# Attention with routed experts on one core: a reciprocal split by a product with ones, epsilon on POOL, loads in pieces, and value products in two groups

## What is computed

```python
x = x + xattn(layernorm(x), ctx, pos, pos, Wq, Wkv, Wout, bout)
x = x + ffn(layernorm(x), gate_w, bias, shared_w1, shared_w3, shared_w2, w1, w3, w2)
# xattn: q = rope(x @ Wq), k = rope(ctx @ Wk), v = ctx @ Wv
#        softmax(q k^T / 4) v @ Wout + bout       per batch and head
# layernorm: (x - mean) / sqrt(var + 1e-5)
```

## Time and profile before

| | us |
|---|---|
| median of 3 runs | 675.25 |
| lowest and highest | 674.48, 675.48 |
| the profiled execution | 673.13 |
| its span, first to last instruction | 671.4 |
| busy: PE, DVE, POOL, ACT | 613.1 (91%), 491.8 (73%), 378.6 (56%), 371.0 (55%) |

### The profile page before, as it was taken

How to read it: one execution, slowest core, us unless ns; L and a number is a source line. 1 busy time by engine, 2 the same in 40 slices (tenths; PEclk the granted TensorE clock), 3 DMA queues, 4 the chain that set the end, 5 groups by cost and what they waited for, 6 DMA issues and landing times.

```text
span 671.4 us, 17296 instructions
## 1 busy us (share of the span) xinstructions
PE 613.1 (91%) x6016; PEld 366.1 (55%) x6016; DVE 491.8 (73%) x944; ACT 371.0 (55%) x620; POOL 378.6 (56%) x423
## 2 busy tenths in 40 slices
PE   2587889999999999779999999999989999999991
PEld 0244445555555555455656566666656666666660
DVE  7478879999999998766476937667655776776771
ACT  4265636666666666764411126666655765765760
POOL 4856657777777776522000013567557477777662
PEclk9879989999999999989999999999999999999996
DMA  8735745555655446513332822765887955446842
GB/s 300 226 68 98 207 91 131 128 124 129 124 126 128 120 111 159 114 50 120 133 95 93 310 96 76 210 192 95 235 258 201 257 93 88 79 90 164 247 83 34
DMA packets 108882, 95.37 MB, mean 142 GB/s; under 512 B 72544, under 2 KB 77152, under 8 KB 108832
## 3 DMA queue, kind: packets, MB, share of 16 engines
q1 hardware_dynamic: 97184, 68.15, 36.8%
q0 software_dynamic: 8752, 20.71, 15.7%
q10 hardware_dynamic: 2896, 5.85, 2.5%
HBM read 70.12 MB, written 23.07 MB: 139 GB/s over the span
## 4 chain that ended last, share of the span: by engine, by line
PE 78%; DVE 6%; DMA 5%; issue 4%; POOL 3%; ACT 1%; SPq 1%; POOLq 0%; DVEq 0%; ACTq 0%
PE p_sc L754 14%; PE p_sc L723 13%; PE p_qk L723 12%; PE p_qk L538 9%; PE p_v L538 9%; PE p_pv L625 5%; PE p_sc L586 3%; PE p_sc L607 3%; PE p_tr L717 2%; PE p_pv L741 2%; DMA used_twice_too<-used_twice 2%; PE p_sc L610 2%; DMA xeT<-xn2T_dram 1%; DMA xe<-xn_dram,from_at 1%; DVE negmax L1128 1%
## 5 line engine op out<-in xcount | busy, mean ns | idle before, releaser
L1128 DVE TENSOR_REDUCE negmax<-p_sc 128x4 f16<-128x512 f32 x128 | 81.0, 683 | 19.0 <-PE p_sc L586 18.3
L849 ACT ACTIVATE prob<-p_sc 128x512 f32<-128x512 f32 x128 | 69.5, 600 | 24.7 <-PE p_sc L610 20.6
L980 ACT CAST hiddenT<-p_pv 128x384 f16<-128x384 f32 x54 | 25.8, 478 | 99.5 <-PE p_pv L741 99.5
L1530 POOL COPY from_at<-from_rows 128x1 uint32 (+1 forms) x40 | 31.7, 791 | 80.2 <-DVE from_rows L1375 76.9
L1550 POOL DMA_INDIRECT out<-prob,to_at x38 | 68.2, 1796 | 10.8 <-issue 10.4
L754 PE MATMUL p_sc<-used_twice,hiddenT 128*128 128x512 f16 (+1 forms) x306 | 71.7, 379 | 0.0
L723 PE MATMUL p_qk<-used_twice,xeT 128*128 128x352 f16 x420 | 68.4, 313 | 0.2 <-DMA xeT<-xn2T_dram 0.2
L723 PE MATMUL p_sc<-used_twice,xeT 128*128 128x352 f16 x420 | 68.4, 312 | 0.0
L1255 DVE TENSOR_TENSOR hidden<-p_sc,act_g 128x352 f32<-128x352 f32 x55 | 28.8, 524 | 51.2 <-PE p_sc L723 29.1
L959 ACT COPY xeT<-p_tr 128x1024 f16<-128x1024 f16 x40 | 40.5, 1012 | 37.0 <-PE p_tr L717 37.0
L538 PE MATMUL p_qk<-used_twice,xnT 128*128 128x512 f16 x192 | 53.7, 407 | 5.5 <-DVE used_twice L1097 3.8
(11 more groups left out here) (178 smaller groups left out, 1417.9 us busy)
## 6 DMA issues: line engine op xcount, KB each, us to landing
w<-e SPq DMA_DIRECT2D x20, 1408.0 KB
w<-e SPq DMA_DIRECT2D x20, 512.0 KB
out<-stream SPq DMA_DIRECT2D x17, 256.0 KB, 2.5
values<-weighed SPq DMA_DIRECT2D x32, 128.0 KB, 2.0
xn_dram<-xn_parts SPq DMA_DIRECT2D x16, 256.0 KB, 2.0
xn2T_dram<-xn2T SPq DMA_DIRECT2D x16, 256.0 KB, 2.2
w<-e SPq DMA_DIRECT2D x20, 192.0 KB
xeT<-xn2T_dram SPq DMA_DIRECT2D x14, 256.0 KB, 2.7
```

The costliest lines, as they stand in the source:

```text
L849: act.activation(prob[:, c % RING, :], p_scored(c)[:], ACT.Exp, scale=SCALE).then_inc(exp_ready, 1)
L1128: dve.tensor_reduce(negmax[:, c % 2, at:at + CH], p_scored(c)[:].rearrange("p (h t) -> p h t", t=P), AX_X, ALU.max, negate=True).then_inc( ...
L1530: pool.tensor_copy(from_at[:, par, u:u + 1], from_rows[:, bass.ds(q, 1)]).then_inc(from_copied, 1)
```

## The change

- `sums_invert`: the high part is the product of the reciprocal with a tile of fp16 ones instead of a maximum with itself.
- `ln`: DVE no longer adds epsilon. POOL adds it from a constant tile and then takes the power, with a wait between the two. The DVE memsets in `ln` go to columns of their own.
- x is loaded in three pieces: batches 4 and 5 (512 KB) where the one DMA was, 6 to 10 (1280 KB) at the end of ACT's pass 2, and 11 to 15 (1280 KB) at the end of its pass 3.
- The shared expert's weights come in seven pieces over passes 4 to 7: 352 KB of w13 in each and 256, 256 and 192 KB of w2 in the first three.
- For batch 0 only, `q_sum` and `q_low` run on DVE in pass 1, right behind `q_turn`, and no longer on POOL in pass 2.
- Before the first pass DVE makes all four low chunks of wq and turns the first k after them.
- On PE, `shifted_scores` 2 stands ahead of the second half of the value projection, `shifted_scores` 3 behind it, then `weigh_values` 0 and 1 back to back; `weigh_values` 2 and 3 are back to back behind chunk 1 of the query projection.

```diff
-                pe.wait_ge(ln1_step, b * 4 + 4)
+                pe.wait_ge(ln1_step, b * 3 + 3)
...
                 on(-3, spread_recip)
+                on(-2, shifted_scores, 2)
                 on(-1, project_v, 1)
-                on(-2, shifted_scores, 2)
+                on(-2, shifted_scores, 3)
                 on(-2, weigh_values, 0)
-                on(-2, shifted_scores, 3)
                 on(-2, weigh_values, 1)
                 on(0, project_q, 0)
                 on(-5, xn2_transpose)
                 on(-1, scores, 0)
+                on(0, project_q, 1)
                 on(-2, weigh_values, 2)
-                on(0, project_q, 1)
                 on(-2, weigh_values, 3)
...
-            act.dma_start(stream[:, 4:B, :], x_t[:, 4:B, :]).then_inc(x_late, 16)
+            act.dma_start(stream[:, 4:6, :], x_t[:, 4:6, :]).then_inc(x_late, 16)
...
-                if isinstance(b, int) and b == 4:
+                if isinstance(b, int) and 4 <= b < 4 + KC:
                     act.wait_ge(w_lo, KCC + 2 * KC)
-                    act.dma_start(w13[:, 0], s13.rearrange("(c p) n -> p c n", p=P)).then_inc(w_shared, 16)
-                    act.dma_start(w2[:, 0, 0:2, :], s2[0:2 * P].rearrange("(c p) n -> p c n", p=P)).then_inc(w_shared, 16)
-                    act.dma_start(w2[0:ICH[2][1], 0, 2, :], s2[2 * P:INNER]).then_inc(w_shared, 16)
+                    act.dma_start(w13[:, 0, b - 4], s13[(b - 4) * P:(b - 3) * P]).then_inc(w_shared, 16)
+                if isinstance(b, int) and 4 <= b < 4 + len(ICH):
+                    i, k = ICH[b - 4]
+                    act.dma_start(w2[0:k, 0, b - 4], s2[i:i + k]).then_inc(w_shared, 16)
+                if isinstance(b, int) and b in (2, 3):
+                    rows = slice(6, 11) if b == 2 else slice(11, B)
+                    act.dma_start(stream[:, rows, :], x_t[:, rows, :]).then_inc(x_later[b - 2], 16)
...
-                    dve.wait_ge(step, base + 2)
-                    dve.tensor_scalar(mv[:, 1:2], mv[:, 1:2], EPS, None, ALU.add).then_inc(step, 1)
...
+            def q_sum(b, par):
+                dve.wait_ge(turned_q, b * 3 + 3)
+                dve.tensor_tensor(rot[:, 0:DIM], rot[:, 0:DIM], swp[:, 0:DIM], ALU.add).then_inc(q_rot, 1)
+
+            def q_low(b, par):
+                dve.wait_ge(q_hi, b + 1)
+                dve.tensor_tensor(q_part[:, :, :, 1, :], twice_each(rot[:, 0:DIM]), q_part[:, :, :, 0, :], ALU.subtract).then_inc(q_parts, 1)
...
-                dve.tensor_tensor(recip16[0:HEADS], recip[:], recip[:], ALU.max).then_inc(recip_step, 1)
+                if not later(b, 1):
+                    dve.wait_ge(consts, 1)
+                dve.tensor_tensor(recip16[0:HEADS], recip[:], ones16[0:HEADS, :], ALU.mult).then_inc(recip_step, 1)
...
-            weights_low(wq16, wq_in, range(2), KCC)
+            weights_low(wq16, wq_in, range(KC), KCC)
             k_turn(0, 0)
-            weights_low(wq16, wq_in, range(2, KC), KCC)
...
                 on(-1, q_turn)
+                if isinstance(b, int) and b == 1:
+                    q_sum(0, 0)
+                    q_low(0, 0)
...
+                pool.tensor_tensor(to[:], mv[:, 1:2], eps_of[:], ALU.add).then_inc(eps_added, 1)
+                pool.wait_ge(eps_added, b + 1)
+                pool.tensor_tensor(to[:], to[:], minus_half[:], ALU.pow).then_inc(ready, 1)
...
-            pipeline(step, pool, 0, B + 5, 8, (B - 8) // 2, ahead=[rstd1_make, ctx_low])
+            pipeline(step, pool, 0, B + 5, 8, (B - 8) // 2, ahead=[rstd1_make, ctx_low, q_sum, q_low])
```

More of the change, by code:

```diff
@@ L114, in build @@
         ones16 = sb("ones16", [P, P], F16)
-        carrier_dve, carrier_pool = sb("carrier_dve", [P, 1]), sb("carrier_pool", [P, 2 * SUB + 1])
-        minus_half = sb("minus_half", [P, 1])
+        carrier_dve, carrier_pool = sb("carrier_dve", [P, 3]), sb("carrier_pool", [P, 2 * SUB + 1])
+        minus_half = sb("minus_half", [P, 1]); eps_of = sb("eps_of", [P, 1])
         angle = sb("angle", [P, B, ROT])
@@ L871, in xn2_high @@
             def xn2_high(b, par):
-                act.wait_ge(ln2_step, b * 5 + 5)
+                act.wait_ge(ln2_step, b * 4 + 4)
                 if later(b, 1):
@@ L891, in split_shared13 @@
             def split_shared13():
-                act.wait_ge(w_shared, 3 * 16)
+                act.wait_ge(w_shared, (KC + len(ICH)) * 16)
                 act.wait_ge(q_done, B)
@@ L1070, in ln1_stats @@
                     dve.wait_ge(x_next, 16)
-                else:
-                    dve.wait_ge(x_late, 16)
-                ln(ln1_step, 4, 0, b, row(b), stats1, mv1, rstd1_ready, rstd1, xn[:], "stats")
+                elif not later(b, 6):
+                    dve.wait_ge(x_late, 16)
+                else:
+                    for half in x_later:
+                        dve.wait_ge(half, 16)
+                ln(ln1_step, 3, 0, b, row(b), stats1, mv1, rstd1_ready, rstd1, xn[:], "stats")
             def ln1_norm(b, par):
@@ L1077, in ln1_norm @@
                     dve.wait_ge(xnT_done, b)
-                ln(ln1_step, 4, 0, b, row(b), stats1, mv1, rstd1_ready, rstd1, xn[:], "norm")
+                ln(ln1_step, 3, 0, b, row(b), stats1, mv1, rstd1_ready, rstd1, xn[:], "norm")
             def ln2_stats(b, par):
-                dve.wait_ge(ln2_step, b * 5 + 1)
-                dve.memset(carrier_dve[:], 0.0)
-                ln(ln2_step, 5, 1, b, row(b), stats2, mv2, rstd2_ready, rstd2, xn2[:, par, :], "stats")
+                dve.wait_ge(ln2_step, b * 4 + 1)
+                dve.memset(carrier_dve[:, 2:3], 0.0)
+                ln(ln2_step, 4, 1, b, row(b), stats2, mv2, rstd2_ready, rstd2, xn2[:, par, :], "stats")
             def ln2_norm(b, par):
@@ L1087, in ln2_norm @@
                     dve.wait_ge(xn2_lo, b - 1)
-                ln(ln2_step, 5, 1, b, row(b), stats2, mv2, rstd2_ready, rstd2, xn2[:, par, :], "norm")
+                ln(ln2_step, 4, 1, b, row(b), stats2, mv2, rstd2_ready, rstd2, xn2[:, par, :], "norm")
             def xnT_low(b, par):
@@ L1163, in split_shared13 @@
             def split_shared13(chunks):
-                dve.wait_ge(w_shared, 3 * 16)
+                dve.wait_ge(w_shared, (KC + len(ICH)) * 16)
                 for c in chunks:
@@ L1429, in _, with rstd @@
         def _(pool):
-            def rstd(step, need, to, mv, ready):
+            def rstd(b, step, need, to, mv, eps_added, ready):
                 pool.wait_ge(step, need)
-                pool.tensor_tensor(to[:], mv[:, 1:2], minus_half[:], ALU.pow).then_inc(ready, 1)
+                pool.tensor_tensor(to[:], mv[:, 1:2], eps_of[:], ALU.add).then_inc(eps_added, 1)
+                pool.wait_ge(eps_added, b + 1)
+                pool.tensor_tensor(to[:], to[:], minus_half[:], ALU.pow).then_inc(ready, 1)
             def rstd1_make(b, par):
-                rstd(ln1_step, b * 4 + 3, rstd1, mv1, rstd1_ready)
+                rstd(b, ln1_step, b * 3 + 2, rstd1, mv1, eps1_added, rstd1_ready)
             def rstd2_make(b, par):
-                rstd(ln2_step, b * 5 + 4, rstd2, mv2, rstd2_ready)
+                rstd(b, ln2_step, b * 4 + 3, rstd2, mv2, eps2_added, rstd2_ready)
             def ctx_low(b, par):
@@ L1444, in _ @@
             pool.memset(minus_half[:], -0.5).then_inc(cleared, 1)
+            pool.memset(eps_of[:], EPS).then_inc(cleared, 1)
             pool.memset(ident[:], 0.0).then_inc(cleared, 1)
             pool.memset(ident16[:], 0.0).then_inc(cleared, 1)
-            pool.wait_ge(cleared, 3)
+            pool.wait_ge(cleared, 4)
             for m in (ident, ident16):
@@ L1450, in _ @@
                                    pattern=[[-1, P]], channel_multiplier=1).then_inc(cleared, 1)
-            pool.wait_ge(cleared, 5)
+            pool.wait_ge(cleared, 6)
             pool.nop().then_inc(ident_ready, 1)
@@ L1473, in spread_make @@
                                        pattern=[[-4, 4], [0, HD], [-HEADS // 2, 2]], channel_multiplier=1).then_inc(cleared, 1)
-                pool.wait_ge(cleared, 19 + 4 * part)
+                pool.wait_ge(cleared, 20 + 4 * part)
             def row(b):
```

14 lines of the change are left out of this document (7 added, 7 removed).

## The result

The changed kernel takes 665.79 us (median of 4 runs, 663.14 to 667.02) against 675.35 us for the kernel before on the same chip: a ratio of 0.986, 95% interval 0.982 to 0.990. The forecast was 663.8 us with a range of 657.5 to 669.5. The profiled execution took 665.54 us, 663.8 of them span.

The account below looks back on a forecast made before the run. The steady pass was taken to be a closed circle through PE, ACT, POOL and DVE. Terms 4.1 + 0.4 + 5.1 - 0.8 + 2.0 + 0.7 = 11.5 us took the median from 675.25 to 663.8 us, range 657.5 to 669.5.

Parts of the forecast that it names:

- The order on PE: Steady attention passes: reordering PE's groups takes a pass from 16.06 to 15.7 us, 4.1 us over 11 passes.
- The joins: Back-to-back `weigh_values` calls on PE: each join saves between 0 and 0.21 us, taken as 0.13.
- the branch over `ctx_high` and `ctx_low`: ACT and POOL in the steady pass: late next, not shortened, only 0.37 us of idle ahead of `k_low` to gain.
- The stalled pass: Pass with the weight load at 79.47: falls to 15.7 us with the weights in pieces, 5.1 us gained.
- The pieces' price: x pieces in passes 2 and 3, with ACT's issues and the moved `weigh_values` 0: 0.8 us charged, between 0 and twice 4.8.
- out of the way when q's transposes start: A 608 KB piece takes 2.3 us, is issued ahead of `q_low` (2.13), and so does not delay q's transposes.
- signs of being wrong: PE idling ahead of `weigh_values` 2, `k_low` idling as before, or passes 2 to 7 waiting for transposes.
- The slower rival: Pieces hold q's transposes for their full time, 17.5 us, giving 680.5 us; pieces in the way 0.07, slower than before 0.03.
- The start: First q on DVE and wq before k: first scores at 30.3 to 31.5 instead of 32.88, 2.0 us gained.
- The third rival: Idle time elsewhere moves the slow clock; not spelled out in the prediction given, which lists start-up over 3 us off, 0.09.
- The product with ones and epsilon: Product on DVE still waits for POOL's `q_low`; epsilon adds fit POOL's idle time: both costed at nothing on the circle.
- The end of attention: At 284.48 PE's 1.44 us wait for a half turned after `shifted_scores` 3, now 0.9 earlier: 0.7 us gained.

Follow-up runs that it names:

- b_order: Kernel before with PE's new order alone, all loads whole: median 667.13 us, ratio 0.989, steady pass 15.50 us.
- b_pieces: Kernel before with both loads (late x and shared weights) in pieces alone: median 673.36 us, ratio 0.998, steady pass 16.07 us.
- a_two_xw: Changed kernel with wo's high part made ahead of `k_high` in pass 2, weight pieces issued behind `k_high`, late x in one DMA: 660.84 us, ratio 0.984.
- a_wo: Changed kernel with ACT making the output weights' high part ahead of `k_high` in pass 2 instead of at the pass's end: 664.20 us, ratio 0.988.
- a_early: Changed kernel with the pieces of x and weights issued behind `k_high` instead of behind `q_high`: 662.03 us, ratio 0.985.
- b_firstq: Kernel before with the first q finished on DVE and wq before k, alone: 672.69 us, ratio 1.000.
- b_recip: Kernel before with the product with ones alone: 672.96 us, ratio 0.999, steady pass 16.07 us.
- a_no_eps: Changed kernel with the two epsilon adds back on DVE: 666.16 us, ratio 0.989, steady pass 15.50 us.

## Why the prediction was right, and where it was not

**The order on PE: right in mechanism, a little small.** Forecast 15.7 us, measured 15.51, and b_order shows that nothing else is needed for it. The joins were put at 0.13 us and the pair of value products gives 0.12. PE's floor was put at 15.4, and PE is busy 19.96 of 20 us in a pass of 15.51; the idle time of 0.3 that it was to regain did not come. The term that was mis-sized is the branch over `ctx_high` and `ctx_low`: from the start of `exp` 4 (207.87 in ACT's timeline) to `ctx_low` are 211.32 - 207.87 = 3.45 us, where the earlier trace rows give 3.65, and the wait of `ctx_low` for ACT went from 0.82 to 0.71. By my count none of this could shrink. These 0.20 and the 0.37 of idle time that was forecast make 0.57; the pass lost 0.55. Whether PE or this branch sets the 15.51 can't be told: neither has slack. Over the passes 4.1 were forecast and 3.64 - 0.20 = 3.44 came, in passes 5 to 13 and in pass 4. b_order, without pieces, has 4.14 + 0.15 = 4.29 there, so the pieces took about 0.8.

**The stalled pass: right, the size in part by luck.** 5.1 forecast, 5.60 measured, and b_pieces alone takes 5.28 from it. But the stalled pass takes 17.88 to 22.26 us in the four traces with whole loads, by the wait and the clock that it has, and the forecast took the one of 20.76 for granted.

**The pieces' price: too low.** I charged 0.8 us. Scores wait 1.87, 0.58, 0.55 and 0.91 us, 3.91 in sum; without the 0.78 and 0.75 that b_order waits in passes 2 and 6 with whole loads, 2.4 are left for the pieces. a_two_xw, which differs from a_wo in x and in the place of the issues alone, ends attention 278.01 - 275.15 = 2.86 us sooner, 1.03 of them in pass 6. So the price is 2 to 3 us. The step that failed is "out of the way when q's transposes start": SP's queue shows the first halves' pair 1.0 us later behind two pieces, 608 KB together. Of the prediction's own signs of being wrong, waits for transposes in passes 2 to 7 did come, in four of them. The slower rival had the right mechanism, at 2 to 3 of its 17.5 us; its point of decision was 12.3. The Trainium skill ("DMA: Bandwidth & Descriptors", Bandwidth) advises against small batches. By that rule the weights in pieces, of 192 to 352 KB, should have been the costly part. No run shows that: in a_early the same sizes, issued earlier in the pass, leave waits of 0.71 and 0.36 us in passes 2 and 5 and none in pass 4, where there were 1.87, 0.55 and 0.58.

**The start: wrong.** The first projection (17.1 forecast, 16.84 measured), DVE's end of the first q (27 to 28.2, measured 27.55) and the first scores (30.3 to 31.5, measured 30.81) all came out. The step that failed is the last one: I took the gain at the first scores as a gain of the kernel. From there the way leads over the first exponential, which stands on ACT behind the next batch's `q_high`, the 2.18 us of output weights and a table load, and `q_high` waits for POOL, which still had one-off work (a 2.75 us `spread` constant ahead of `k_low`). That way got only 1.4 us shorter; the rest became the wait of 3.97 us, and the low clock behind that wait took the 1.4. The prediction reads rows of PE, DVE and POOL there and none of ACT. a_wo and b_firstq show it from both sides. Of the forecast 2.0 us, 3.80 - 4.01 = -0.2 arrived. The third rival, by which idle time in other places moves the slow clock, described a part of this.

**The product with ones and epsilon: right,** both nothing, by b_recip and a_no_eps. One detail was small: DVE's wait for the power is 0.41 us, not 0.1, and still costs nothing.

**The end of attention: wrong in place, and near in size by luck.** The wait of 1.44 us in the earlier trace rows is still 1.17. What fell in pass 15 is the wait of the transpose of the maxima, from 2.41 us before (first fence below) to 1.41 after:

```profile
290.06 0.23 PE L596 MATMUL p_tr<-ident,negmax 128*128 128x128 f16 x1 [2.41 <-DVE negmax L1128]
```

```profile
280.78 0.23 PE L596 MATMUL p_tr<-ident,negmax 128*128 128x128 f16 x1 [1.41 <-DVE negmax L1141]
```

b_order and b_firstq have the short wait too (1.42 each), b_pieces and b_recip the long one (2.37 and 2.40). The difference lies on DVE, ahead of the last two maxima, in two low parts of the shared weights (before, then after):

```profile
286.12 2.68 DVE L1160 SCALAR_TENSOR_TENSOR used_twice<-w,used_twice 128x704 f16<-128x704 f32 x2
```

```profile
277.84 1.68 DVE L1175 SCALAR_TENSOR_TENSOR used_twice<-w,used_twice 128x704 f16<-128x704 f32 x2
```

They take 2.64 to 2.68 us in the three traces with the long wait and 1.68 or 1.69 in the other eleven. POOL's `xn2_low` starts while they run. Where they are long it takes 1.15 to 1.20 us, and where they are short 1.43 to 1.91. So one of the two waited for the other, and which one did is not settled by the order on PE: b_firstq has the old order and the short wait.

**The sum.** 11.5 us were forecast; attention gave 9.28. The start is 2.2 us short, pass 2 and passes 4 to 13 about 1.1; the stall and the end (passes 14 and 15) brought 0.5 and 0.6 more than forecast. The medians, 9.56 us apart, are near the attention phase, while the profiled executions are 7.6 apart, since the rest, nearly all experts, took 1.68 us more in one than in the other. The total came out nearer than its terms did.

## What to carry to other kernels

A gain at the start of a pipeline is followed to the first instruction that every later pass depends on, on each engine, before it is booked; one-off work placed right ahead of it on another engine takes the gain, and moving that work into idle time gives it back. The long waits on PE had a stretch of low clock with them in most of these traces, so the two are counted together. In this pass, with PE busy 99% of the time, reordering PE's own groups gave the whole steady gain, and the product with ones on DVE and epsilon on POOL gave nothing. A load that is cut up needs a place in the pass as well as a size: issue it where no transfer that the bound engine waits for is about to start. And before a difference of 1 or 2 us between two traces is put down to an edit, look whether work ahead of the edit already differs.

## What the runs showed of the hardware

- Two groups of fp32 matmuls on tiles of 32 columns, back to back instead of apart, save about 0.12 us on PE beside the idle time between them.
- The output weights' low parts on DVE (four 128x512, both inputs in SBUF) took 5.06 us in the changed kernel against 3.57 in the kernel before. That DVE waits there for POOL's `q_low` and the `k_sum` behind it fits the two timelines; it was not tried alone.
- The same twelve matmuls of the first query projection took 4.08 to 5.28 us in fourteen profiles; 5.26 and 4.09 in two kernels which are alike up to there, both with the granted clock at 1.00 in that stretch.
- The stretch behind the last transpose of the maxima, nearly all the same code of experts, took 377.2 to 384.4 us in fourteen profiles, 2% apart, with the granted clock at its lower level for 11 to 14 us near the end in each. A single profiled execution can't tell a change of 3 us in a kernel of this length; a phase of it can.
